# A fused vision block: a gating product two tiles later, two moves one tile earlier, and a last stage with fewer small matmuls

## What is computed

```python
# third part: Mamba over windows of 8 x 8 points (D_INNER 128, D_STATE 16)
xz = seq @ W_in;  x, z = split(xz)
x  = silu(causal_conv4(x) + conv_b)
dt, Bm, Cm = split(x @ W_xproj);  dt = softplus(dt @ W_dt + b_dt)
h  = exp(dt * A) * h + (dt * x) * Bm        # for each of 64 steps
y  = (h * Cm).sum(states) + x * Dp
out = (y * silu(z)) @ W_out                 # the gating product

# fourth part: 32 experts (EC), each takes its best 8 tokens of an image
logits = layernorm(t) @ gate_w.T + gate_b   # softmax over the tokens, top 8
pooled = (gathered * topv).sum(k)
h   = gelu(concat(pooled, 1) @ weight1[e])  # 65 x 256; the 1 brings the bias row
out = concat(h, 1) @ weight2[e]
outputs.at[chosen tokens].add(out * topv)
```

## Time and profile before

| what | value |
|---|---|
| median of 3 runs | 8435.43 us (8434.6 to 8456.22) |
| the profiled execution | 8443.99 us, of which the profile's span is 8442.2 us |
| stage B, 2480 to 8000 us of the span | DVE busy 5163.61 of 5520 us, POOL 5104.32, PE 3864.80, ACT 3647.77 |
| stage B, TensorE's granted clock | 0.81 of full speed |
| stage C, 8080 to 8442 us | PE busy 237.18 of 362 us, DVE 176.76 |

### The profile page before, as it was taken

How to read it: one execution, slowest core, us unless ns; L and a number is a source line. 1 busy time by engine, 2 the same in 40 slices (tenths; PEclk the granted TensorE clock), 3 DMA queues, 4 the chain that set the end, 5 groups by cost and what they waited for, 6 DMA issues and landing times. The chain is left out here.

```text
span 8442.2 us, 102482 instructions
## 1 busy us (share of the span) xinstructions
PE 6257.6 (74%) x30638; PEld 2416.4 (29%) x30638; DVE 6790.0 (80%) x7951; ACT 4334.5 (51%) x5972; POOL 5192.9 (62%) x1730
## 2 busy tenths in 40 slices
PE   6888888888885776777777777766777767777647
PEld 3444444444441222222222222222222222222212
DVE  3555555555556999999999999999999999999954
ACT  1222222222224666666666666666666666666621
POOL 0000000000006999999999999999999999999820
PEclk8988989989887888888888888888888888888757
DMA  1111111111114656656656656556656556556556
GB/s 31 44 41 43 46 38 45 39 45 38 46 35 153 206 187 204 202 187 203 204 187 205 201 190 207 198 187 204 203 188 209 199 192 204 199 190 204 193 112 231
DMA packets 514969, 1253.48 MB, mean 148 GB/s; under 512 B 170312, under 2 KB 172524, under 8 KB 513900
## 3 DMA queue, kind: packets, MB, share of 16 engines
q1 hardware_dynamic: 514092, 1249.20, 45.5%
q10 hardware_dynamic: 320, 3.21, 0.2%
q0 software_dynamic: 512, 0.53, 0.0%
HBM read 943.30 MB, written 231.21 MB: 139 GB/s over the span
## 5 line engine op out<-in xcount | busy, mean ns | idle before, releaser
L1186 DVE TENSOR_TENSOR_SCAN b_h<-b_a,b_h 128x448 f32<-128x448 f32 x3584 | 3672.5, 1073 | 104.0 <-ACT b_a L1115 98.1
L1024 POOL TENSOR_TENSOR b_h<-b_h,b_ct 128x1792 f32<-128x1792 f32 x896 | 3570.4, 3988 | 272.3 <-DVE b_h L1186 259.1
L1115 ACT ACTIVATE b_a<-b_dts,decay 128x441 f32<-128x441 f32 x3584 | 2225.8, 629 | 1589.1 <-DVE b_h L1186 1562.2
L1036 POOL MEMSET b_seq<- 128x938 f32 x2 | 1.7, 880 | 2480.2 <-POOLq L799 2480.2
L1176 DVE TENSOR_TENSOR b_h<-b_dus,b_b 128x896 f32<-128x896 f32 x1344 | 1433.4, 1067 | 61.9 <-DMA b_dus<-d_dtu 61.1
L1283 PE MATMUL b_b<-b_rows,spread_b 16*128 16x512 f32 (+1 forms) x1792 | 566.4, 651 | 888.3 <-DVE b_h L1176 887.3
L1010 POOL TENSOR_TENSOR b_h<-b_dus,b_bt 128x896 f32<-128x896 f32 x448 | 933.6, 2084 | 50.6 <-DMA b_bt<-d_rows 30.5
L1291 PE MATMUL b_y<-b_h,fold 128*32 128x512 f32 (+1 forms) x7168 | 952.1, 658 | 8.1 <-POOL b_h L1024 8.1
L496 DVE TENSOR_TENSOR a_xg<-a_xd,a_pb 128x784 f32<-128x784 f32 x512 | 495.1, 967 | 506.6 <-PE a_pb L610 504.5
L1252 PE MATMUL b_w<-b_seq,w_conv 128*128 128x384 f32 (+1 forms) x896 | 550.6, 777 | 12.6 <-DMA b_seq<-b_seq 12.6
L1244 PE MATMUL b_w<-b_u,wx 128*64 128x512 f32 x448 | 360.9, 961 | 211.5 <-DVE b_dt L1208 211.5
(11 more groups left out here) (225 smaller groups left out, 8539.4 us busy)
## 6 DMA issues: line engine op xcount, KB each, us to landing
b_bt<-d_rows SPq DMA_DIRECT2D x448, 448.0 KB, 6.0
b_ct<-d_rows SPq DMA_DIRECT2D x448, 448.0 KB, 3.9
b_dts<-d_dt SPq DMA_DIRECT2D x448, 448.0 KB, 5.7
b_dus<-d_dtu SPq DMA_DIRECT2D x448, 448.0 KB, 6.3
a_xd<-a_xn SPq DMA_DIRECT2D x256, 196.0 KB, 3.4
d_dt<-b_dt SPq DMA_DIRECT2D x112, 448.0 KB, 2.5
d_dtu<-b_soft SPq DMA_DIRECT2D x112, 448.0 KB, 2.7
b_seq<-b_seq SPq DMA_DIRECT2D x112, 234.0 KB, 6.7
```

The source lines that it names most:

```text
L1024: nc.gpsimd.tensor_tensor(two, two, ct[t // 4 % 2][:].unsqueeze(1).broadcast_to([P, 2, TB]), ALU.mult).then_inc(hc_done, 2)
L1115: a(steps(bank(aa, k)), steps(half(dts[t % 4], k)), ACT.Exp, scale=decay[:, t % 4, t // 4:t // 4 + 1]).then_inc(a_done, 1)
L1186: v.tensor_tensor_scan(half(hh[t], k), bank(aa, k), half(hh[t], k), 0.0, ALU.mult, ALU.add).then_inc(h_done, 1)
```

## The change

In stage B three operations stand elsewhere in the hand-written order: DVE's gating product goes from tile 5 to tile 7, before `step`; ACT's move of the gate logits from tile 13 to 12, and of the tokens from 15 to 14. In stage C the bias of a group of four experts is one matmul with a spread one-hot matrix, 128 columns wide, instead of four 4-column ones, and the transposes are done after each half, with a hidden buffer of half the size.

```diff
-                                if t == 13 and finals:
+                                if t == 12 and finals:
                                     act.wait_ge(lg_stored, 16 * (it - 1))
                                     move(spot(1, "lgp", it, kind), lg[:], ACT.Identity, rows=2 * EC, bias=b_gate[:])
-                                if t == 15 and finals:
+                                if t == 14 and finals:
                                     act.wait_ge(tok_stored, 32 * (it - 1))
                                     move(spot(1, "tok", it, kind), tok[:])
...
-                                if t == 5 and not (kind == FIRST and i == 0):
+                                if t == 7 and not (kind == FIRST and i == 0):
                                     gated(1 - i, row_no(i, 0, it) - 1, unit_no(i, it) - 1)
...
+                spread_e = sb("spread_e", [EC, EC, 32])
...
-                hid_t = sb("hid_t", [P, NQ, HID])
+                hid_t = sb("hid_t", [P, NQ // 2, HID])
...
                                 at = q % (NQ // 2) * HID
+                                mm(ph[:, at:at + HID], spread_e[:, 4 * q:4 * q + 4, :].rearrange("e g j -> e (g j)"), w1b[:], start=(q % 2 == 0), stop=False)
+                            for q in range(NQ // 2 * half, NQ // 2 * (half + 1)):
+                                at = q % (NQ // 2) * HID
                                 for g in range(4):
                                     x = 4 * q + g
                                     h = slice(C * half, C * half + C)
-                                    dst = ph[32 * g:32 * g + IMG, at:at + HID]
-                                    mm(dst, by_expert[h, x, :], w1[h, x % (EC // 2), :], start=True, stop=False)
-                                    last = mm(dst, by_e[:, :, x], w1b[:], start=False, stop=True)
+                                    last = mm(ph[32 * g:32 * g + IMG, at:at + HID], by_expert[h, x, :], w1[h, x % (EC // 2), :],
+                                              start=False, stop=(q % 2 == 1))
...
                             if n == 19:
+                                turn_hidden(1, 0)
                                 hidden(1, 1)
                             if n == 21:
-                                turn_hidden(1)
+                                turn_hidden(1, 1)
```

More of the change, by code:

```diff
@@ L1496, in _ @@
                         nc.gpsimd.memset(by_e[:], 0.0).then_inc(places, 1)
-                        pool.wait_ge(places, 2)
+                        nc.gpsimd.memset(spread_e[:], 0.0).then_inc(places, 1)
+                        pool.wait_ge(places, 3)
                         for g in range(4):
@@ L1500, in _ @@
                                                     pattern=[[4, NQ], [-1, R]], channel_multiplier=EC).then_inc(places, 1)
-                            pool.wait_ge(places, g + 3)
+                            pool.wait_ge(places, g + 4)
                         nc.gpsimd.affine_select(out=by_e[:], in_=by_e[:], compare_op=ALU.not_equal, fill=1.0, base=0,
                                                 pattern=[[0, IMG], [-1, EC]], channel_multiplier=1).then_inc(places, 1)
-                        pool.wait_ge(places, 7)
+                        nc.gpsimd.affine_select(out=spread_e[:], in_=spread_e[:], compare_op=ALU.not_equal, fill=1.0, base=0,
+                                                pattern=[[-1, EC], [0, 32]], channel_multiplier=1).then_inc(places, 1)
+                        pool.wait_ge(places, 9)
                         for t in range(NT):
@@ L1537, in gelu @@
                             act.wait_ge(h_ready[t], half + 1)
-                            a(hid_t[:, NQ // 2 * half:NQ // 2 * (half + 1), :].rearrange("p q h -> p (q h)"), ph[:],
-                              ACT.Gelu).then_inc(gelu_ready[t], 1)
+                            if half:
+                                act.wait_ge(ht_ready[t], half)
+                            elif t:
+                                act.wait_ge(ht_ready[t - 1], 2)
+                            a(hid_t[:].rearrange("p q h -> p (q h)"), ph[:], ACT.Gelu).then_inc(gelu_ready[t], 1)
                         def turned(t):
-                            act.wait_ge(ht_ready[t], 1)
+                            act.wait_ge(ht_ready[t], 2)
                             a(hid[:].rearrange("p k m -> p (k m)"), hid_p, ACT.Copy).then_inc(hid_ready[t], 1)
@@ L1681, in hidden, with turn_hidden @@
                                     h = slice(C * half, C * half + C)
-                                    dst = ph[32 * g:32 * g + IMG, at:at + HID]
-                                    mm(dst, by_expert[h, x, :], w1[h, x % (EC // 2), :], start=True, stop=False)
-                                    last = mm(dst, by_e[:, :, x], w1b[:], start=False, stop=True)
+                                    last = mm(ph[32 * g:32 * g + IMG, at:at + HID], by_expert[h, x, :], w1[h, x % (EC // 2), :],
+                                              start=False, stop=(q % 2 == 1))
                             last.then_inc(h_ready[t], 1)
[L1687 to L1690, removed]
+                        def turn_hidden(t, half):
+                            pe.wait_ge(gelu_ready[t], half + 1)
+                            for m in range(NQ):
+                                n = NQ * half + m
+                                last = mm(hid_p[:, 4 * IMG * n:4 * IMG * (n + 1)], hid_t[:, m // 2, P * (m % 2):P * (m % 2) + P], some_of,
                                           start=True, stop=True)
@@ L1711, in _ @@
                         pe.wait_ge(w_loaded, 128)
-                        pe.wait_ge(places, 7)
+                        pe.wait_ge(places, 9)
                         turn(0)
                         hidden(0, 0)
+                        turn_hidden(0, 0)
                         hidden(0, 1)
-                        turn_hidden(0)
+                        turn_hidden(0, 1)
                         products(0, 0, NQ)
```

3 lines of the change are left out of this document (1 added, 2 removed).

## The result

The changed kernel took 8658.91 us in the median of 4 runs (8653.77 to 8668.32), the kernel before 8435.51 (8434.6 to 8456.22): a ratio of 1.026, with a 95% interval of 1.0242 to 1.0278. The forecast was 8735 us, +302 on its profiled execution; +223 was measured. The loss is in stage B, where VectorE (DVE) now waits longer for two other engines; stage C gives a part of it back.

What follows compares the result with a forecast made beforehand. DVE was taken to bound stage B, with the scans of tile 5 set by ACT; 109 + 255 - 70 + 20 + 33 - 45 = +302 us on the profiled execution gave 8735 us, 3.6% slower, own range 8560 to 8890.

Steps and rivals of the forecast that it cites:

- The product at tile 5 costs nothing: Stage B: the product lies in a gap DVE has anyway, waiting for ACT's exponential; removing it there gains 0.
- the waits are real: Rival, tile 5: the product holds up the scans, so its wait would go, -123 us; about 8220 us, chance 0.05.
- The product's own time, +109: Tile 7, where DVE waited for nothing: the product costs 0.98 us in 111 units, +109 us.
- PE behind the product, +255: Stage B: skip and b_b queue behind the product at half clock; DVE waits 2.3 us at tile 9, 111 times.
- full clock at skip: Rival: PE runs skip at full clock, so DVE's input of tile 9 does not wait; about 8480 us, chance 0.10.
- lower case: Tile 9: skip slow but b_b fast, b_b ready at S + 5.5 (S: product's start), DVE waits 1.5 us.
- fourth rival: The new clock costs less: PE returns to full clock within skip, wait 1.0 us; about 8590 us, chance 0.09.
- Moves and convolution, -70 + 20 + 33 = -17: Stage B: tokens at tile 14 save 70 us, logits at tile 12 cost 20, the convolution's clock costs 33.
- The +20 for the logits: Gate logits moved at tile 12 make the scans of tile 13 a little late, 0.35 us in 55 turns: +20 us.
- the +33 for the convolution's clock: Convolution with i = 0: PE pauses longer before b_b and partly loses clock, 0.6 us 55 times: +33 us.
- Stage C, -45: Hidden layer: 20 matmuls a half instead of 32, transposes moved at no cost: -45 us (25 to 55).
- 12 fewer save 11.3: Stage C: at 0.94 us per small matmul at half clock, 12 fewer save 11.3 us in each half.

Runs made afterwards that it cites:

- e5: Kernel before with the gating product behind the input of tile 6, still before the scans of tile 5: 8449.71 us, 0.9999.
- e6: Kernel before without the gating product; a one-column copy that does not wait for PE stands at tile 5: 8447.99 us, 0.9992.
- e4: Kernel before with the product at tile 7 and PE computing b_b of tiles 8 to 11 ahead of skip: 8542.12 us, 1.0115.
- e2: Kernel before with only the gating product moved from tile 5 to tile 7: 8800.95 us, 1.042.
- e7: e2 plus 24 small unused matmuls on PE between the w_dt_full strip and skip: 8547.71 us, 1.0106 to the kernel before.
- e3: Kernel before with only ACT's two moves one tile earlier (logits at tile 12, tokens at 14): 8429.19 us, 0.9984.
- e9: Kernel before with only ACT's move of the tokens at tile 14, logits staying at 13: 8418.31 us, 0.9967.
- e8: Kernel before with, per four experts, four weight matmuls then four bias matmuls instead of four pairs: 8355.7 us, 0.9893.
- e12: Kernel before with each expert's bias matmul behind the next expert's weight matmul, shapes and column groups alternating: 8448.8 us, 1.0004.
- e1: Stage C as in the change, stage B as in the kernel before: 8372.42 us, 0.9912.
- e11: The change's stage C alone, its small matmuls reordered so four in a row write the same 32 columns: 8385.02 us, 0.9933 to the kernel before.

## Why the prediction was right, step by step

Its sign, its cause and its range held. The terms:

- *The product at tile 5 costs nothing.* Shown. e5 moves it within the gap (0.9999), e6 leaves it out (0.9992). The 123 us before it were ACT's time under another name, and the scans took them over when the product left: 342.1 us after, where the prediction said over 300. The rival "the waits are real" is excluded.
- *The product's own time, +109.* Measured +97 (e4; its interval goes from 67 to 128), +84.5 in stage B.
- *PE behind the product, +255.* Measured 258.8 for the move alone (e2 less e4), and e7 gives 253 of it back by nothing but filled pauses. Skip took 3.30 to 3.35 us behind pauses of 6.58 to 7.06, as priced. The rival "full clock at skip" stands realised in e7. In the changed kernel the term was smaller, and here the forecast had the size wrong: DVE waited 188.4 us for b_b, 1.70 us a unit and not 2.3, where it was 247.9 us, 2.2 a unit, in e2. The slow skip is as priced; "half clock for most of b_b" is not. Of the 111 b_b behind skip 18 took over 1.9 us, in e2 85; most ran at full clock right behind the slow skip (5083.84, 1.12 us). That is the prediction's lower case, and not its fourth rival, whose clock was to return within skip. Stage B of the two kernels differs in ACT's two moves alone. Why the clock comes back earlier with them is not settled; the pauses before skip are the same (739.7 and 743.8 us in all).
- *Moves and convolution, -70 + 20 + 33 = -17.* Measured -14 (e3, not told from zero), -31 in stage B. The sum fits better than its parts, and that is luck: the wait for ACT fell by 60 to 81 us, and most of it was given back where the prediction had nothing, at the product (+19 us in e3, +37 in e9) and at b_dus (+9, and +25 in e9 with the stage's first wait left out). The +20 for the logits and the +33 for the convolution's clock were not measured one by one. The same gap of ACT takes in whatever reaches tile 5 earlier.
- *Stage C, -45.* The term was mis-sized: -79, outside its own 25 to 55. The step "12 fewer save 11.3" took 0.94 us for the price of a 4-column matmul. It was the price of a run of matmuls of one shape, which in the kernel before held one matmul each. Without the bias matmuls between them, sixteen of one shape took 3.6 us, not 15; e8 and e12 show the cause. The fewer matmuls were worth next to nothing: e8 has all 32, a half of 7.8 us for 7.3, and a stage as short (277.6 us for 276.9). That the transposes move at no cost held in the sum only: the waits of DVE's five sums from the first half of t = 1 on are 26.3 us, in e8, where the transposes stay, 28.4.
- *The page "TensorE: Matmul & The Clock Gate" of the Trainium skill (Part 1), against which the earlier trace rows were preferred.* The rows held: the halves at t = 0 ran at half clock after the change as well, and the second half of t = 1 too (3.78 and 3.59 us, as at t = 0). The clock of this term was right; the 0.94 us were not.

The parts add up to 355 - 14 - 74 = +267 us (e2's 0.042, e3's 0.0016 and e1's 0.0088 of 8450). The whole change cost 223. The 44 us between them are as much as the intervals of the three runs leave open (32, 18 and 24 us); the trace shows 59.5 us less wait for b_b in the whole than in e2, which would cover them. The two misses, b_b (188 us for 255) and stage C (79 for 45), went the same way, to a shorter time; it still lies within the range because the range had b_b down to 170.

What the prediction announced of the new profile stood there: no wait at the product, over 300 us before the scans, a new line for b_b, 110 times and 2.5 us at the longest, a pause of 6.6 us and skip of 3.3 us, no wait of the square, none at the scans of tile 1 (5161.99 in the unit above). Not met were the size of the new line (188.4 us, not 250), the 66 us for the four halves (7.3 + 7.3 + 4.4 + 7.3 = 26.3), and one of the sums' two waits of 16 us (6.57). The other, 15.58, has the forecast size by luck: the half is short (7.3 us), and the wait for gelu and the transposes ahead of it (2.7 and 3.4 us) fill it up.

## What to carry to other kernels

A wait in front of an instruction says little on what it costs: look whether the next instruction behind it would have waited anyway, since then the place is free, and any other place is not. When a producer is moved later, read the other engine's queue behind its consumer: what is queued there runs after a pause, and at half clock that is twice as long. Small matmuls that use only parts of the array did best here in runs of one shape, each on another column group; the order was worth more than the count.

## What the runs showed of the hardware

- Four matmuls of 64 rows by 4 columns, or of 32 rows by 4 columns, each on its own group of 32 columns, took 0.97 us from the start of the four to the next four at half clock (e8), as long as one alone does (0.94).
- Alternating between the two shapes, none overlapped, in whatever column group (e12); 0.94 us each.
- With one shape but four in a row on the same column group, sixteen took 8.59 us (e11): between the 3.60 of neighbours apart and the 15 of no overlap.
- Filler matmuls on an idle PE paid for themselves: 613.6 us of them made the kernel 253 us faster (e7 against e2), since skip and b_b behind the pause then ran at full clock (1.77 and 1.12 us for 3.35 and 2.07). Putting b_b ahead of skip did as much without them (e4).
- Behind pauses of 6.58 to 7.06 us the four matmuls of skip ran at half clock in every unit shown; what came next was at half clock in some units and back at full clock in others (1.12 to 2.07 us for the same four matmuls of b_b).
